# Routing tables of two expert stages, made block by block with per-partition scalars

## The reference, cut to what matters

```
# layer 2: one expert per token
router_probs = softmax(x @ gate_w);  expert_idx = argmax(router_probs)
for e in range(8):  out += where(expert_idx == e, expert_w, 0) * (gelu(x @ w1[e] + b1[e]) @ w2[e] + b2[e])
# layer 4: two experts per token
routing_weights, expert_indices = top_k(x @ Wr + br, 2);  softmax over the two
y = (silu(x @ W1[e]) * (x @ W3[e])) @ W2[e];  out = sum over e of c[..., e] * y[..., e]
```

## Time and profile before

| | us |
|---|---|
| median of 3 runs (lowest, highest) | 749.55 (747.85, 751.25) |
| the profiled execution: its time | 752.79 |
| the profiled execution: its span | 751.0 |
| busy in the span: PE | 562.4 |
| busy in the span: DVE | 379.7 |
| busy in the span: ACT | 272.2 |
| busy in the span: POOL | 358.1 |

### The profile page before, as it was taken

How to read it: one execution, slowest core, us unless ns; L and a number is a source line. 1 busy time by engine, 2 the same in 40 slices (tenths; PEclk the granted TensorE clock), 3 DMA queues, 4 the chain that set the end, 5 groups by cost and what they waited for, 6 DMA issues and landing times. The chain is left out here.

```text
span 751.0 us, 37703 instructions
## 1 busy us (share of the span) xinstructions
PE 562.4 (75%) x15566; PEld 488.1 (65%) x15566; DVE 379.7 (51%) x1128; ACT 272.2 (36%) x678; POOL 358.1 (48%) x684
## 2 busy tenths in 40 slices
PE   5785645998996785179987389989951399989992
PEld 4563534888886674179886156667641399979991
DVE  3563841232322591626667046767747545556662
ACT  4553321222321163056654235544411133334331
POOL 4575653753330102568886554300002554587775
PEclk9887655657575695589999589999965599999996
DMA  5001042234221580756553110100003566545550
GB/s 143 2 17 43 27 98 63 76 93 105 67 76 26 177 247 4 143 161 204 175 174 92 43 37 22 29 4 4 5 3 63 138 211 218 211 173 204 209 192 21
DMA packets 78270, 75.10 MB, mean 100 GB/s; under 512 B 33472, under 2 KB 56160, under 8 KB 78160
## 3 DMA queue, kind: packets, MB, share of 16 engines
q1 hardware_dynamic: 73840, 64.45, 28.1%
q0 software_dynamic: 4320, 9.18, 5.2%
HBM read 19.89 MB, written 11.24 MB: 41 GB/s over the span
## 5 line engine op out<-in xcount | busy, mean ns | idle before, releaser
L2014 PE MATMUL e_psH<-spare,e_up_w 128*128 x728 | 99.1, 280 | 2.8 <-DMA e_up_w<-wac 2.6
L2014 PEld LDWEIGHTS e_psH<-spare,e_up_w 128*128 128x128 f32 x728 | 90.4, 196 | 3.8 <-issue 3.6
L2021 PE MATMUL e_psY<-vb,e_hT 128*128 x364 | 57.5, 280 | 5.5 <-DVE e_hT L2179 5.4
L2186 DVE SCALAR_TENSOR_TENSOR e_row<-e_psY,e_row 128x128 f32 x91 | 32.0, 351 | 46.1 <-issue 25.0
L646 POOL TENSOR_TENSOR tb<-tinv,mb 128x128 f32<-128x128 f32 x64 | 24.4, 403 | 63.2 <-PE d_psY L684 59.9
L1327 ACT ACTIVATE e_hT<-e_psH,e_b 128x128 f32<-128x128 f32 x156 | 44.6, 369 | 25.8 <-PE e_psH L1283 25.8
L2021 PEld LDWEIGHTS e_psY<-vb,e_hT 128*128 128x128 f32 x364 | 47.8, 191 | 8.5 <-issue 7.9
L1231 POOL DMA_INDIRECT e_row<-xe_dram,e_read_at x39 | 42.5, 1090 | 15.6 <-issue 6.7
L810 DVE TENSOR_TENSOR S<-d_psS,on 128x64 f32<-128x64 f32 x64 | 14.4, 225 | 68.7 <-PE d_psS L748 68.1
L2179 DVE TENSOR_TENSOR e_hT<-e_pre,e_psH 128x256 f32<-128x256 f32 x91 | 37.4, 411 | 19.3 <-ACT e_pre L2078 14.4
L2078 ACT ACTIVATE e_pre<-e_psH 128x256 f32<-128x256 f32 x91 | 33.7, 377 | 36.0 <-PE e_psH L2014 35.0
(11 more groups left out here) (371 smaller groups left out, 1415.3 us busy)
## 6 DMA issues: line engine op xcount, KB each, us to landing
e_up_w<-wac SPq DMA_DIRECT2D x91, 256.0 KB
e_up_w<-wa SPq DMA_DIRECT2D x39, 256.0 KB
xe_dram<-xe SPq DMA_DIRECT2D x2, 2192.0 KB, 14.4
vk_now<-vk SPq DMA_DIRECT2D x16, 192.0 KB, 2.1
outs_dram<-spare SPq DMA_DIRECT2D x39, 64.0 KB
r<-in_L_attn_hidden_states SPq DMA_DIRECT2D x8, 256.0 KB, 4.8
wa<-in_L_ffn_w SPq DMA_DIRECT2D x1, 2048.0 KB, 9.8
wac<-in_L_ffn_W SPq DMA_DIRECT2D x2, 1024.0 KB, 9.2
```

Source lines behind the costliest of these rows:

```text
L2014: mm = nc.tensor.matmul(psH[i % 3][:, f], up_w[i % WDEEP][:, f * P:(f + 1) * P], xT[:, bass.ds(t, 1)].rearrange("p a l -> p (a l)"), start ...
L2021: mm = nc.tensor.matmul(psY[i % 3][:, 0:D], hT[i % DEEP][:, k], wb[:, bass.ds(e * NF + k, 1)].rearrange("p a d -> p (a d)"), start=(k == 0 ...
L2186: v.scalar_tensor_tensor(z, psY[i % 3][:, 0:D], flat_row[:, bass.ds(t * XW + at + D, 1)], z, ALU.mult, ALU.add).then_inc(z_done, 1)
```

## The change

In both routings is_col and col_h are dropped. at_col and at_pos are made block by block: GpSimd compares the column numbers with the block's own `col`, one value to a partition, and multiplies with the block's `code`, in one operation of 39 or 32 columns; VectorE compares the position numbers with the block's `pos_h` in one operation of 128 columns. That is 32 operations on each engine in each routing in place of four. The scalars (pos_h, code) become fp32. Only the last of each eight raises the semaphore, so PE still waits for groups of eight. GpSimd waits for `split` at 1, which pos_h now raises.

```diff
@@ stage_single
-        col_h, pos_h = tmp("col_h", [P, BLOCKS], F16), tmp("pos_h", [P, BLOCKS], F16)
-        col_no, pos_no, code = tmp("col_no", [P, TILES], F16), tmp("pos_no", [P, P], F16), tmp("code", [P, BLOCKS], F16)
-        at_pos, is_col, at_col = tmp("at_pos", [P, BLOCKS, P], F16), tmp("is_col", [P, BLOCKS, TILES], F16), tmp("at_col", [P, BLOCKS, TILES], F16)
+        pos_h = tmp("pos_h", [P, BLOCKS])
+        col_no, pos_no, code = tmp("col_no", [P, TILES], F16), tmp("pos_no", [P, P], F16), tmp("code", [P, BLOCKS])
+        at_pos, at_col = tmp("at_pos", [P, BLOCKS, P], F16), tmp("at_col", [P, BLOCKS, TILES], F16)
...
-                pool.wait_ge(split, 2)
-                for c in range(BLOCKS // CUT):
-                    n = slice(c * CUT, c * CUT + CUT)
-                    pool.tensor_tensor(at_col[:, n], is_col[:, n], spread(code[:, n], TILES), ALU.mult).then_inc(hot_col, 1)
+                pool.wait_ge(split, 1)
+                for n in range(BLOCKS):
+                    ins = pool.tensor_scalar(at_col[:, n], col_no[:, :], col[:, n:n + 1], code[:, n:n + 1], ALU.is_equal, ALU.mult)
+                    if n % CUT == CUT - 1:
+                        ins.then_inc(hot_col, 1)
...
-                v.scalar_tensor_tensor(pos_h[:, :], col[:, :], -float(P), slot[:, :], ALU.mult, ALU.add)
-                v.tensor_copy(col_h[:, :], col[:, :]).then_inc(split, 1)
+                v.scalar_tensor_tensor(pos_h[:, :], col[:, :], -float(P), slot[:, :], ALU.mult, ALU.add).then_inc(split, 1)
                 dve.wait_ge(split, 1)
-                v.tensor_tensor(is_col[:, :, :], every(col_no[:, :], BLOCKS), spread(col_h[:, :], TILES), ALU.is_equal).then_inc(split, 1)
                 for c in range(BLOCKS // CUT):
-                    n = slice(c * CUT, c * CUT + CUT)
-                    v.tensor_tensor(at_pos[:, n], every(pos_no[:, :], CUT), spread(pos_h[:, n], P), ALU.is_equal).then_inc(hot, 1)
+                    for n in range(c * CUT, c * CUT + CUT):
+                        ins = v.tensor_scalar(at_pos[:, n], pos_no[:, :], pos_h[:, n:n + 1], None, ALU.is_equal)
+                    ins.then_inc(hot, 1)
@@ stage_chain: the same in its declarations, on GpSimd and on VectorE
                 def hot_rows(c):
-                    n = slice(c * CUT, c * CUT + CUT)
-                    return v.tensor_tensor(at_pos[:, n], every(pos_no[:, :], CUT), spread(pos_h[:, n], P), ALU.is_equal)
+                    for n in range(c * CUT, c * CUT + CUT):
+                        ins = v.tensor_scalar(at_pos[:, n], pos_no[:, :], pos_h[:, n:n + 1], None, ALU.is_equal)
+                    return ins
```

More of the change, by code:

```diff
@@ L1839, in stage_chain @@
         slot, col = tmp("slot", [P, BLOCKS]), tmp("col", [P, BLOCKS])
-        col_h, pos_h = tmp("col_h", [P, BLOCKS], F16), tmp("pos_h", [P, BLOCKS], F16)
-        col_no, pos_no, code = tmp("col_no", [P, BLOCKS], F16), tmp("pos_no", [P, P], F16), tmp("code", [P, BLOCKS], F16)
-        at_pos, is_col, at_col = tmp("at_pos", [P, BLOCKS, P], F16), tmp("is_col", [P, BLOCKS, BLOCKS], F16), tmp("at_col", [P, BLOCKS, BLOCKS], F16)
+        pos_h = tmp("pos_h", [P, BLOCKS])
+        col_no, pos_no, code = tmp("col_no", [P, BLOCKS], F16), tmp("pos_no", [P, P], F16), tmp("code", [P, BLOCKS])
+        at_pos, at_col = tmp("at_pos", [P, BLOCKS, P], F16), tmp("at_col", [P, BLOCKS, BLOCKS], F16)
         read_at = tmp("read_at", [P, BLOCKS], U32)
@@ L1960, in _ @@
                 pool.tensor_tensor(gates, gates, spread(rcp[:, :], E), ALU.mult).then_inc(weighed, 1)
-                pool.wait_ge(split, 2)
-                for c in range(BLOCKS // CUT):
-                    n = slice(c * CUT, c * CUT + CUT)
-                    pool.tensor_tensor(at_col[:, n], is_col[:, n], spread(code[:, n], BLOCKS), ALU.mult).then_inc(hot_col, 1)
+                pool.wait_ge(split, 1)
+                for n in range(BLOCKS):
+                    ins = pool.tensor_scalar(at_col[:, n], col_no[:, :], col[:, n:n + 1], code[:, n:n + 1], ALU.is_equal, ALU.mult)
+                    if n % CUT == CUT - 1:
+                        ins.then_inc(hot_col, 1)
                 def gather(t):
@@ L2150, in _ @@
                 link(v.tensor_scalar(col[:, :], col[:, :], ROUND, -ROUND, ALU.add, ALU.add))
-                v.scalar_tensor_tensor(pos_h[:, :], col[:, :], -float(P), slot[:, :], ALU.mult, ALU.add)
-                v.tensor_copy(col_h[:, :], col[:, :]).then_inc(split, 1)
+                v.scalar_tensor_tensor(pos_h[:, :], col[:, :], -float(P), slot[:, :], ALU.mult, ALU.add).then_inc(split, 1)
                 dve.wait_ge(split, 1)
-                v.tensor_tensor(is_col[:, :, :], every(col_no[:, :], BLOCKS), spread(col_h[:, :], BLOCKS), ALU.is_equal).then_inc(split, 1)
                 for c in range(BLOCKS // CUT):
```

## The result

The change makes the kernel slower. On one chip, run in turn, the kernel after took 763.98 us (median of four, 760.79 to 768.46) and the kernel before 750.40 us (median of four, 747.85 to 753.50): ratio 1.0183, 95% interval 1.0106 to 1.0261, or 8 to 20 us. The forecast was 750.1, in a range up to 755.5.

The account below looks back on a forecast made before the run. The prediction took routing 2 to be bound by its tables and routing 1's first gather by the store of xe. Routing 2 at +0.57 us and routing 1 at 0 gave 750.1 us from 749.55, range 746.8 to 755.5.

Parts of the forecast that it names:

- GpSimd's term: at_col as 32 GpSimd operations at 0.26 us a step; by it read_at of routing 2 ends at 590.4.
- The one-scalar row of 0.268: Profile row for GpSimd with one per-partition scalar, 0.268 us, used in pricing an at_col step at 0.26.
- Upper bound: the slowest 128x32 row, 0.436: Upper bound for one GpSimd at_col step, 0.436 us, from the slowest 128x32 row of the profile before.
- the slack of routing 1: Routing 1, read_at to first gather: the gather waits for the store of xe, leaving 2.6 us to cover later tables.
- VectorE's term: at_pos as 32 VectorE operations at 0.24 us a step; read_at of routing 2 ends 0.57 us later.
- the lower bound from rows, 0.144: VectorE's at_pos step at least 0.144 us: an 8-column per-partition scalar operation, 0.224, with neighbours overlapping by 0.08.
- Rival C: Both engines take turns at the tables' memory, 0.45 us a step, 10.9 us lost, 760.5 us; chance 0.17.
- The argument against C: Of GpSimd's 1.5 us operation of 256 columns only 0.42 showed on VectorE; the new ones have 32 or 39 columns.
- B: Small table operations are cheap on both engines, 0.144 and 0.217 us; total 747.7 us; chance 0.21.
- D: Only the tables hold the gathers, so the whole saving, 2.5 and 3.6 us, reaches the end: 743.5 us; chance 0.04.

Follow-up runs that it names:

- the probe: Kernel before plus 48 extra GpSimd operations on scratch tiles behind its last scatter, nothing beside them, in groups of three of one form; 775.99 us, run once.
- VectorE's half alone: Kernel before with only at_pos cut into 32 short VectorE operations; is_col and GpSimd's four tensor_tensor kept; 751.51 us, ratio 1.0005.
- long operations: Kernel before with all tables on VectorE in few long fp16 operations, block number innermost, constants laid out by GpSimd; 749.64 us, ratio 0.9962.

## Why the prediction was wrong

- **The failed step is GpSimd's term.** "I take 0.26": it measured 0.47 in routing 2 (15.18 less one operation, over 31) and 0.50 in routing 1. It was priced from rows of multiply and add with constants, or with one scalar on a single column, and of "the second such scalar and the overlap of neighbours" it says: "I let them cancel". Nothing cancelled. In the probe, at 32 columns, the two per-partition scalars together cost 0.14 to 0.16 us over constants (379 - 236 in fp32, 475 - 318 in fp16), and the compare 0.08 to 0.11 over multiply and add; the compare wasn't named as a cost at all. The one-scalar row of 0.268 is of a single column, where the probe has 0.38 to 0.42 for one scalar on 32.
- **The bound was too low, and not used.** "Upper bound: the slowest 128x32 row, 0.436" lies below the median of the operation, 0.472. And the prediction did not carry it on: by its own steps read_at in routing 2 moves by 581.32 + 32c + 0.8 - 590.51 = 32c - 8.39, and the gather in routing 1 by 305.66 + 32c + 0.8 + 0.27 - 317.48 = 32c - 10.75, at c = 0.436 by 5.6 and 3.2 us, which makes 758.3; the range stopped at 755.5, because a GpSimd alone at that bound stood among no rival.
- **The structure held.** The same two sums with the measured steps give 32 x 0.474 - 8.39 = 6.8 (measured 6.76) and 32 x 0.503 - 10.75 = 5.3 at routing 1's gather (measured 5.42, 17.52 for 12.10 from pos_h). GpSimd starts 0.11 us behind pos_h, read_at ends 0.76 behind the tables (0.78 predicted), the slack of routing 1 is what was read (2.6 us). The work from the first expert matmul on moved as a block, to within 0.9 us.
- **VectorE's term was too large.** 0.24 predicted, 0.167 measured; it no longer mattered. By its sum alone read_at of routing 2 would have come earlier: 32 x 0.167 - 7.11 = -1.8. The Trainium skill's estimate, 0.094 ("VectorE: DVE Perf Modes", section on the TRN2 errata), was too small; here the lower bound from rows, 0.144, was the nearest.
- **Rival C had the size and not the cause.** Its 760.5 lies nearest to the result, by luck: it put 0.45 on both engines. But the two engines don't run at one period (0.167 and 0.47), and GpSimd keeps 0.45 when VectorE is done. Beside VectorE the first ten steps of routing 2 take 5.2 us (starts at 583.53 to 588.71) for 4.5 at the later pace: turns are 0.7 us of 6.8. The argument against C also rested on a misread row: the 1.5 us of GpSimd's old operation of 256 columns was mostly waiting beside VectorE's long ones, for in VectorE's half alone it takes 0.61. So the change replaced 2.3 us of GpSimd's own work (4 in 2.32) with 15.
- **B and D** had short steps on both engines. That one engine would be cheap and the other dear was left out, though PE waits for the later of the two.
- The rule on the shared port (the Trainium skill, "SBUF — State Buffer", section "SBUF: two separate sides") was cited for C: whichever comes first holds the other out for a whole instruction. The runs agree where GpSimd runs a tensor_tensor or a memset (at_pos held to 662 ns; e_count held 2.29 us, until the memset ended) and where VectorE runs long two-input operations (at_col held 3,635 ns). They don't agree for the change itself, where VectorE passed 0.47 us operations of GpSimd at 0.167 a step.

Left open: what GpSimd does in the time that the scalars and the compare cost; the trace shows whole operations only.

## What to carry to other kernels

Price a small operation from a row that has the same engine, the same operation (a compare is not a multiply) and the same kind of scalars; where no such row exists, put the upper bound through the whole sum, by itself, before the range is drawn. Where a consumer waits for tables of two engines, cutting the work of both into 32 pieces pays only if it pays on the slower of them. A long duration beside another engine may be waiting: read the operation's price where the neighbour is short or idle. And before shortening what stands ahead of a wait, read what else ends at that wait: here a store left 1.3 of 3.5 us in routing 2, and in routing 1 the tables were hidden behind it.

## What the runs showed of the hardware

- On GpSimd a compare costs 3.2 to 3.4 ns a column, multiply and add 0.9; two per-partition scalars cost 0.14 to 0.16 us an operation. The Trainium skill, "GPSIMD Engine Reference", section "Engine selection", has operations of one input there at roughly line rate; one rate doesn't fit both, for a compare takes over three times as long a column as multiply and add.
- On VectorE the same compare-and-multiply of 32 columns took 0.21 us a step, under half of GpSimd's 0.45 to 0.50.
- An fp16 operation of two inputs on 1024 columns takes 0.69 us when the innermost step of every operand is one, and 1.22 as in the kernel before, where one operand repeats a value along it.
- PE's load of a 128x128 fp16 weight table took 152 to 170 ns when its elements lie eight apart in memory, 104 to 110 when they lie side by side (long operations, and before).
- A memset on GpSimd held a VectorE operation of 8 columns for 2.29 us (0.17 before), until 0.03 us after the memset's end, in a place where the store hid it. It is a single case.
